# Passing first-choice results through the second choices' rows: a GNN and mixture-of-experts kernel with one scatter less per token

## The chip, the cores and the metric

The kernel runs on one core of one Trainium2 chip. The time is that of the device, in microseconds, from the start of one execution to its end. The median of three runs of the kernel before is 489.01 us (488.24 to 489.42).

## The reference

8192 tokens of 128 features, in 128 graphs of 64 nodes, pass through two residual blocks. All is float32.

```python
x = x + gnn(layernorm(x), adj)     # adjacency product, 128->512, RMS norm, SiLU, 512->128
x = x + ffn(layernorm(x))          # mixture of 8 experts, each token uses its 2 best

def ffn(xf):
    top_w, top_i = top_k(xf @ Wg + bg, 2)
    top_w = softmax(top_w)
    w_dense = sum(one_hot(top_i, E) * top_w[..., None], axis=1)
    for e in range(E):
        h = gelu(xf @ W1[e] + b1[e])
        out = out + w_dense[:, e:e+1] * (h @ W2[e] + b2[e])
```

Below, `x2` is the sum after the first block. A token's result is `x2` plus its first choice's weighted output plus its second choice's weighted output.

## The kernel before, in words

There are two stages. In the token stage a loop over 16 groups of 512 tokens (`s`, with each step working on several groups at once) computes the first block, the gate scores, the two best experts of each token and, by prefix sums on TensorE (`prefix`), a row number for each token and choice. For each choice k there is an array in HBM, `dispatched_rows{k}`, with a region for each expert. GpSimd scatters each token's row to it with an indirect DMA of 128 rows, `dispatch(g, j, k)`. A row holds the token's number, the two weights, mean and reciprocal deviation for the second layer norm, and x2: 133 numbers, 532 bytes. That is 4 dispatches a group and choice, 128 in all. The first choices' dispatches of a group follow it by two steps. The second choices' ones are spread, three a step from step 3 on, and the other 22 between the tiles of the next stage (`second(n)`).

In the expert stage a tile is 128 rows of one expert. There are 71 tiles (TILES) for the first choices, numbered 0 to 70, and 71 for the second choices, 71 to 141 (NT = 142). Which expert and which row a tile begins with stands in tables that VectorE computes: `early_row` and `early_expert` for the first 40 tiles (EARLY), which can be full tiles of the first 12 groups and so start before all is dispatched; `row_tab` and `expert_tab` for the others. Places of a region's last tile that hold no token are padded with rows whose token number is out of bounds (`pad`), so that their writes are dropped.

The work of a tile i on its engines, each with its own queue in program order:

- SyncE, `load_slots(i)`: waits until slot buffer i % 16 (RING) is free, which is when the write of tile i - 16 has landed (`added`), reads the tile's row from the table, and loads 128 rows to `slot_rows`.
- VectorE: `norm_slots(i + 4)` (L1035), `copy_block(i + 3)` (L1029, first-layer weights and biases of the tile's expert), then `finish(i)`: L1115 adds the bias to the second layer's result, and L1122 (first choices: times weight, plus x2) or L1125 (second choices: times weight) writes `y_out`.
- TensorE: transpose of tile i + 1 (L661), first layer of tile i (L668, 4 matmuls), second layer of tile i - 1 (L683, 4 matmuls). A float32 matmul stands as two records in the trace.
- ScalarE: copies the transpose, and applies Gelu.
- GpSimd, `write_tile(i)`: L437, an indirect DMA that scatters 128 results of 512 bytes to `out`, for the first choices; L440, the same with an addition to what is in `out`, for the second choices. An addition must not start before the first choice's result of the same token is there, so GpSimd waits for all first choices' writes ahead of tile 71 (`wait_written`).

The end of the kernel waits on SyncE for all writes.

## Time and profile before

| what | us |
|---|---|
| median of the runs | 489.01 |
| the profiled execution, its own time | 488.13 |
| its span, first to last instruction | 486.2 |
| TensorE busy (matmul) | 465.9, 96% of the span |
| VectorE busy | 354.1 |
| GpSimd busy | 353.4 |
| 71 accumulating writes, L440 | 112.6, 1.586 each |
| 71 plain writes, L437 | 72.2, 1.017 each |
| 128 dispatches, L425 | 126.0, 0.985 each |

Start with the end of the span and go back: what is the last thing that runs, and since when is it alone. Then ask for each stretch which engine has no idle time. GpSimd's share of 73% is an average over stretches: it is busy 8 tenths of each slice in the last third, up to the last slice, in which all other engines are still. The TensorE clock granted is full in all slices but the last.

### The profile page before, as it was taken

To read this page: it belongs to the slowest core of one execution; us is meant where nothing else is said; L and a number is where in the kernel's file an instruction comes from. 1 tells how busy PE (TensorE), PEld (TensorE's weight loads), DVE (VectorE), ACT (ScalarE), POOL (GpSimd) and SP (SyncE) were. 2 spreads that over 40 slices of the span, in tenths; PEclk is the share of its full clock that TensorE was granted. 3 is DMA by queue.
4 is the path that set the end of the run, shared out by engine and by line. 5 is a ranking of instruction groups with operands and counts; after the bars stand their busy time and mean duration, and the time that the engine had idled before them with its cause. 6 is when DMAs were issued, how large, how long until landed. Compare 5 with 4: busy or idle time off the path is not lost.

```text
span 486.2 us, 14184 instructions
## 1 busy us (share of the span) xinstructions
PE 465.9 (96%) x3715; PEld 422.8 (87%) x3715; DVE 354.1 (73%) x1484; ACT 264.2 (54%) x830; POOL 353.4 (73%) x310
## 2 busy tenths in 40 slices
PE   8999999999999999999999999999999999999960
PEld 6788888778888777899999999999999999999950
DVE  6798888888887675888867777777667676776730
ACT  2333333333333324677777777777777777777730
POOL 3232587877778777777777777777588888888884
PEclk9999999999999999999999999999999999999995
DMA  6995122222222212323334333333254555555430
GB/s 188 361 320 168 56 79 73 79 77 64 68 64 68 78 40 74 86 70 90 96 91 108 100 104 98 93 85 99 47 68 68 72 72 76 70 69 73 56 33 5
DMA packets 54436, 44.78 MB, mean 92 GB/s; under 512 B 9506, under 2 KB 46024, under 8 KB 54360
## 3 DMA queue, kind: packets, MB, share of 16 engines
q1 hardware_dynamic: 36480, 26.11, 20.0%
q0 software_dynamic: 16592, 17.13, 17.5%
q8 instruction: 35, 0.57, 0.5%
q10 hardware_dynamic: 1288, 0.62, 0.4%
q14 instruction: 41, 0.34, 0.2%
HBM read 25.49 MB, written 19.25 MB: 92 GB/s over the span
## 4 chain that ended last, share of the span: by engine, by line
PE 67%; POOL 15%; issue 14%; DVE 1%; ACT 1%; POOLq 1%
PE ps L683 14%; PE ps L668 14%; POOL out_y L440 14%; PE ps L589 11%; PE ps L575 10%; PE ps L541 3%; PE ps L549 3%; PE ps L582 3%; PE ps L557 2%; PE ps L661 2%; PE ps L567 1%; POOL dispatched_rows L425 1%; PE ps L500 1%; POOLq L71 1%; PE ps L612 0%
## 5 line engine op out<-in xcount | busy, mean ns | idle before, releaser
L775 ACT ACTIVATE gelu_t<-ps,block_w 128x128 f32<-128x128 f32 x568 | 162.5, 369 | 35.1 <-PE ps L668 34.7
L425 POOL DMA_INDIRECT dispatched_rows<-payload,row_idx x128 | 126.0, 985 | 37.3 <-issue 36.7
L668 PE MATMUL ps<-slot_t,block_w 128*128 128x128 f32 x1136 | 150.1, 275 | 0.6 <-ACT slot_t L769 0.6
L683 PE MATMUL ps<-experts,gelu_t 128*128 x1136 | 150.3, 275 | 0.4 <-ACT gelu_t L775 0.3
L683 PEld LDWEIGHTS ps<-experts,gelu_t 128*128 128x128 f32 x1136 | 138.2, 192 | 0.8 <-issue 0.8
L668 PEld LDWEIGHTS ps<-slot_t,block_w 128*128 128x128 f32 x1136 | 138.0, 192 | 0.9 <-ACT slot_t L769 0.9
L440 POOL DMA_INDIRECT out_y<-y_out,slot_rows x71 | 112.6, 1586 | 23.3 <-issue 23.3
L437 POOL DMA_INDIRECT out_y<-y_out,slot_rows x71 | 72.2, 1017 | 24.1 <-issue 19.0
L1115 DVE TENSOR_TENSOR y_bias<-ps,block_w 128x128 f32<-128x128 f32 x142 | 41.3, 291 | 52.8 <-PE ps L683 48.1
L1029 DVE COPY block_w<-experts 128x644 f32 x142 | 73.6, 519 | 2.0 <-issue 2.0
L1035 DVE TENSOR_SCALAR slot_n<-slot_rows 128x128 f32<-128x128 f32 x142 | 58.5, 413 | 15.5 <-DMA slot_rows<-dispatched_rows 15.1
L589 PE MATMUL ps<-w2e,hidden 128*128 128x136 f32 x512 | 69.6, 279 | 0.0
L589 PEld LDWEIGHTS ps<-w2e,hidden 128*128 128x128 f32 x512 | 63.9, 190 | 0.0
L732 ACT ACTIVATE hidden<-ps,vec_cols 128x512 f32<-128x512 f32 x64 | 44.0, 687 | 32.8 <-PE ps L575 32.7
L575 PE MATMUL ps<-agg_r,w1b 128*128 128x512 f32 x128 | 59.1, 603 | 0.0
L769 ACT COPY slot_t<-ps 128x128 f32<-128x128 f32 x142 | 37.7, 266 | 34.4 <-PE ps L661 34.2
L414 POOL TENSOR_TENSOR powers<-powers_in,neg_half 128x12 f32<-128x12 f32 (+2 forms) x17 | 33.9, 1993 | 23.9 <-DVE powers_in L838 23.2
L575 PEld LDWEIGHTS ps<-agg_r,w1b 128*128 128x128 f32 x128 | 23.0, 190 | 22.6 <-issue 22.5
L661 PE MATMUL ps<-ident,slot_n 128*128 128x128 f32 x142 | 38.6, 273 | 0.0
L745 ACT ACTIVATE agg<-ps,ones 128x512 f32<-128x512 f32 x16 | 11.0, 687 | 50.4 <-PE ps L541 50.4
L582 PEld LDWEIGHTS ps<-ident_wg,xs_t 128*128 128x128 f32 x128 | 20.5, 190 | 13.9 <-issue 13.9
L1125 DVE TENSOR_SCALAR y_out<-y_bias,slot_rows 128x128 f32<-128x128 f32 x71 | 30.7, 432 | 2.5
(146 smaller groups left out, 413.3 us busy)
## 6 DMA issues: line engine op xcount, KB each, us to landing
slot_rows<-dispatched_rows SPq DMA_DIRECT2D x142, 66.5 KB
xs<-in_x SPq DMA_DIRECT2D x16, 256.0 KB, 6.5
xs_t<-in_x_t SPq DMA_DIRECT2D x16, 256.0 KB, 3.1
experts<-in_f_w SPq DMA_DIRECT2D x16, 256.0 KB, 5.3
out_y<-y_out,slot_rows POOLq DMA_INDIRECT x142, 3.2
adj_in<-in_adj_t SPq DMA_DIRECT2D x16, 128.0 KB, 4.3
dispatched_rows<-payload,row_idx POOLq DMA_INDIRECT x128, 2.4
dispatched_rows<-pad_rows SPq DMA_DIRECT2D x18, 66.5 KB
```

The costliest lines, as they stand in the source:

```text
L425: pool.indirect_dma_start(rows[k], bass.IndirectOffsetOnAxis(row_idx[:, g, j * TOP_K + k:j * TOP_K + k + 1], 0), payload[:, g * JT + j, 0: ...
L437: pool.indirect_dma_start(out, token, y_out[:, r, :], None, bounds_check=T - 1, oob_is_err=False).then_inc(added[r], 16)
L440: pool.indirect_dma_start(out, token, y_out[:, r, :], None, bounds_check=T - 1, oob_is_err=False, compute_op=ALU.add).then_inc(added[r], 16)
L575: pe.matmul(bank(n % H_BANKS, 0, GROUP), w1b[:, c * P:(c + 1) * P], agg_r[:, s % 2, :], start=True, stop=True).then_inc(h_done, 1)
L589: mm = pe.matmul(x2_part(j), hidden[:, c, j * P:(j + 1) * P], w2e[:, c, :], start=False, stop=(c == C - 1))
L661: pe.transpose(bank(TURN_BANK + i % 2, 0, P), slot_n[:, i % (AHEAD + 1), :], ident[:]).then_inc(slots_turned, 1)
L668: mm = pe.matmul(bank((2 * i + c // 2) % FH_BANKS, c % 2 * SLOTS, SLOTS), block_w[:, i % BLOCKS, c * P:(c + 1) * P], slot_t[:, i % 2, :], ...
L683: mm = pe.matmul(bank(Y_BANK + i % 2, 0, P), gelu_t[:, i % 2, c, :], experts[:, bass.ds(at + (OW2 + c * P), P)], start=(c == 0), stop=(c = ...
L732: act.activation(hidden[:, c, :], ps[:, (C * s + c) % H_BANKS, :], ACT.Silu, scale=vec_cols[:, GRW + c:GRW + c + 1]).then_inc(hidden_ready, 1)
L775: act.activation(gelu_t[:, i % 2, c, :], ps[:, (2 * i + c // 2) % FH_BANKS, c % 2 * SLOTS:(c % 2 + 1) * SLOTS], ACT.Gelu, bias=block_w[:, ...
L1029: dve.tensor_copy(block_w[:, i % BLOCKS, :], experts[:, bass.ds(at, OW2)]).then_inc(block_ready, 1)
L1035: dve.tensor_scalar(slot_n[:, i % (AHEAD + 1), :], row[:, X2:WID], row[:, MEAN:MEAN + 1], row[:, RSTD:RSTD + 1], ALU.subtract, ALU.mult).t ...
```

## The change

A first choice's result no longer goes to `out`. Instead, the whole slot row with the result behind it (262 numbers, 1048 bytes) is scattered to the row of a new array `forwarded_rows` at which the token's second choice has its place. The place travels in the row (`PLACE`, so a row has 134 numbers). A second choice's tile loads such rows, which hold x2, statistics, weights and the first choice's result, adds its own part on VectorE, and writes the final result to `out` with a plain scatter. The accumulating write and GpSimd's waits for earlier writes are gone.

So that the expert stage needn't stand still between the choices, the second choices of the first four groups (SECOND_GROUPS) are still dispatched from the token stage, 16 dispatches, and give 8 full tiles (SECONDS), 71 to 78. Their slots are loaded from `dispatched_rows1`, and the first choices' results for them come later from `forwarded_rows` by a load of their own, `load_prior`, 512 bytes a row. VectorE keeps their second-layer result in the slot (`take_second`) and closes them later (`close_second`): one at tile 75, then two in each of tiles 76 to 79. The early tables are computed for both choices.

```diff
             def write_tile(i):
                 r = i % RING
                 pool.wait_ge(y_ready, i + 1)
-                token = bass.IndirectOffsetOnAxis(slot_rows[:, r, TOKEN:TOKEN + 1].bitcast(I32), 0)
                 if i < TILES:
-                    pool.indirect_dma_start(out, token, y_out[:, r, :], None, bounds_check=T - 1,
+                    place = bass.IndirectOffsetOnAxis(slot_rows[:, r, PLACE:PLACE + 1].bitcast(I32), 0)
+                    pool.indirect_dma_start(forwarded, place, slot_rows[:, r, :], None, bounds_check=DUMMY - 1,
                                             oob_is_err=False).then_inc(added[r], 16)
                 else:
-                    pool.indirect_dma_start(out, token, y_out[:, r, :], None, bounds_check=T - 1,
-                                            oob_is_err=False, compute_op=ALU.add).then_inc(added[r], 16)
-
-            def wait_written(i):
-                pool.wait_ge(added[i % RING], 16 * (i // RING + 1))
+                    token = bass.IndirectOffsetOnAxis(slot_rows[:, r, TOKEN:TOKEN + 1].bitcast(I32), 0)
+                    pool.indirect_dma_start(out, token, slot_rows[:, r, WID:FWD], None, bounds_check=T - 1,
+                                            oob_is_err=False).then_inc(added[r], 16)
...
-                if s >= SECONDS_FROM:
-                    second(3 * (s - SECONDS_FROM))
+                if 0 <= 2 * (s - SECONDS_FROM) < SECOND_GROUPS * JT:
+                    second(2 * (s - SECONDS_FROM))
+                    second(2 * (s - SECONDS_FROM) + 1)
...
-                n = SECONDS_LEFT + (i - 1) // 5 * 2 + (i % 5 == 3)
-                if i % 5 in (1, 3) and n < G * JT:
-                    second(n)
-
-
-                if TILES - 8 <= i < TILES - 1:
-                    wait_written(2 * i - TILES)
-                    wait_written(2 * i - TILES + 1)
-                if i == TILES:
-                    wait_written(TILES - 2)
-                    wait_written(TILES - 1)
                 write_tile(i)
...
-            sp.wait_ge(second_dispatched, 16 * JT * G)
-            for i in range(TILES, NT):
+            sp.wait_ge(second_dispatched, 16 * JT * SECOND_GROUPS)
+            firsts = [load_slots(i) for i in range(TILES, TILES + SECONDS)]
+
+
+            for i in range(TILES + SECONDS - RING, TILES):
+                sp.wait_ge(added[i % RING], 16 * (i // RING + 1))
+            for i in range(TILES, TILES + SECONDS, 2):
+                load_slots(SECONDS + TILES + (i - TILES) // 2)
+                load_prior(i, firsts[i - TILES])
+                load_prior(i + 1, firsts[i + 1 - TILES])
+            for i in range(TILES + SECONDS + SECONDS // 2, NT):
                 load_slots(i)
...
+                dve.tensor_copy(payload[:, cols(g), PLACE].bitcast(I32),
+                                row_f[:].rearrange("p (j k) -> p j k", k=TOP_K)[:, :, 1])
                 dve.tensor_copy(row_idx[:, g, :], row_f[:]).then_inc(rows_ready, 1)
...
+            def take_second(i):
+
+                dve.wait_ge(y_done, i + 1)
+                dve.tensor_tensor(slot_rows[:, i % RING, X2:WID], ps[:, Y_BANK + i % 2, 0:P],
+                                  block_w[:, i % BLOCKS, OB2:OB2 + P], ALU.add).then_inc(y_chain, 1)
+
+            def close_second(i):
+                row = slot_rows[:, i % RING, :]
+                dve.wait_ge(y_chain, i + 1)
+                if i < TILES + SECONDS:
+                    dve.wait_ge(prior_loaded[i - TILES], 16)
+                dve.scalar_tensor_tensor(row[:, WID:FWD], row[:, X2:WID], row[:, WEIGHT + 1:WEIGHT + 2],
+                                         row[:, WID:FWD], ALU.mult, ALU.add).then_inc(y_ready, 1)
...
+                if i == TILES + 4:
+                    close_second(TILES)
+                if TILES + 5 <= i <= TILES + SECONDS:
+                    close_second(2 * i - TILES - 9)
+                    close_second(2 * i - TILES - 8)
+                if i > TILES + SECONDS:
+                    close_second(i)
```

GpSimd's queue from the last writes of the first choices on; the bracket holds the semaphores waited for. Before:

```order
L437 DMA out_y<-y_out,slot_rows 8192x128 [waits y_ready,added2,added1]
L437 DMA out_y<-y_out,slot_rows 8192x128 [waits y_ready,added4,added3]
L437 DMA out_y<-y_out,slot_rows 8192x128 [waits y_ready]
L440 DMA out_y<-y_out,slot_rows 8192x128 [waits y_ready,added6,added5]
L440 DMA out_y<-y_out,slot_rows 8192x128 [waits y_ready] x70
```

And in the changed kernel, from the last dispatches on:

```order
L472 DMA forwarded_rows<-slot_rows 66688x262 [waits y_ready] x11
L460 DMA dispatched_rows<-payload,row_idx 66688x134 [waits rstd_stored,rows_ready]
L472 DMA forwarded_rows<-slot_rows 66688x262 [waits y_ready]
...
L472 DMA forwarded_rows<-slot_rows 66688x262 [waits y_ready] x57
L476 DMA out_y<-slot_rows 8192x128 [waits y_ready] x71
```

GpSimd no longer waits for writes, and between the tiles only the last group's four dispatches are left, behind tiles 10 to 13.

SyncE's queue at the turn between the choices: the loads of tiles 78 and 79. `TENSOR_LOAD` reads a table. Before:

```order
L290 TENSOR_LOAD row_tab [waits added14]
L290 ISA x2
L341 ISA
L341 DMA slot_rows<-dispatched_rows 128x133
L290 TENSOR_LOAD row_tab [waits added15]
```

And in the changed kernel:

```order
L302 TENSOR_LOAD early_row [waits added14]
L302 ISA x2
L358 ISA
L358 DMA slot_rows<-dispatched_rows 128x134
L302 TENSOR_LOAD row_tab [waits added4,added3,added5,added2,added6,added1,added15,added0]
L302 ISA x2
L361 ISA
L361 DMA slot_rows<-forwarded_rows 128x262
L367 ISA
L367 DMA slot_rows<-forwarded_rows 128x128
L367 ISA
L367 DMA slot_rows<-forwarded_rows 128x128
```

The wait for one write has become a wait for eight (and by the loads ahead of it for all 71), and two loads of priors follow each of four slot loads.

VectorE at tile 76 of the changed kernel; before, a tile had one L1115 and one L1125 in place of the last three rows:

```order
L1068 TENSOR_SCALAR slot_n<-slot_rows 128x128 [waits slots_turned,slots_loaded0]
L1062 ISA [waits y_done,y_chain]
L1062 COPY block_w<-experts 128x644
L291 TENSOR_LOAD expert_tab
L291 ISA x2
L1162 TENSOR_TENSOR slot_rows<-ps,block_w 128x128 [waits y_done]
L1170 SCALAR_TENSOR_TENSOR slot_rows<-slot_rows 128x128 [waits prior_loaded1,y_chain]
L1170 SCALAR_TENSOR_TENSOR slot_rows<-slot_rows 128x128 [waits prior_loaded2,y_chain]
```

The normalisation of tile 80 stands first and waits for its load; two closings that wait for priors stand last.

## Rows read from the trace of the kernel before

**Rows 1.** Busy time by stretch: window, length, PE, PEld, DVE, ACT, POOL, clock, DMA.

```profile
202.00:336.00 134.00, 134.00 (x1208) 133.85 (x1207) 102.42 (x334) 99.04 (x353) 103.60 (x102) 1.00 0.35 95
346.00:470.00 124.00, 123.39 (x1105) 123.02 (x1103) 85.16 (x257) 90.92 (x323) 103.34 (x65) 1.00 0.50 66
```

**Rows 2.** Timeline of the end: start us, length us, engine, line, operation [idle before].

```profile
467.18 2.25 PE L683 MATMUL ps<-experts,gelu_t 128*128 x16
...
469.80 0.29 DVE L1125 TENSOR_SCALAR y_out<-y_bias,slot_rows 128x128 f32<-128x128 f32 x1
470.01 1.55 POOL L440 DMA_INDIRECT out_y<-y_out,slot_rows  x1 [0.30 <-issue]
...
479.28 1.55 POOL L440 DMA_INDIRECT out_y<-y_out,slot_rows  x1 [0.30 <-issue]
```

**Rows 3.** GpSimd's indirect DMAs by line: ns min/median/max, first and last start; landing.

```profile
L437 POOL DMA_INDIRECT out_y<-y_out,slot_rows x71: 978/992/1320, 214.9 to 343.9; - x71
...
DMA to landing us min/median/max: 2.1/2.4/4.2
...
L440 POOL DMA_INDIRECT out_y<-y_out,slot_rows x71: 1549/1554/1657, 346.9 to 479.3; - x71
...
L425 POOL DMA_INDIRECT dispatched_rows<-payload,row_idx x128: 957/962/1262, 47.9 to 317.8; - x128
...
out_y<-y_out,slot_rows POOLq DMA_INDIRECT x6, 2.7
```

**Rows 4.** DMA view, windows 60:178 and 346:470: packets, MB, share; issues, landing.

```profile
q0 software_dynamic: 2336, 4.98, 12.6%
...
dispatched_rows<-payload,row_idx POOLq DMA_INDIRECT x74, 2.4
...
q0 software_dynamic: 9216, 4.01, 36.0%
...
out_y<-y_out,slot_rows POOLq DMA_INDIRECT x65, 3.4
```

**Rows 5.** Timeline at the turn: tile 70's result, tile 79's normalisation and transpose.

```profile
336.01 0.35 DVE L1122 SCALAR_TENSOR_TENSOR y_out<-y_bias,slot_rows 128x128 f32<-128x128 f32 x1
...
343.79 0.39 DVE L1035 TENSOR_SCALAR slot_n<-slot_rows 128x128 f32<-128x128 f32 x1
...
346.85 0.27 PE L661 MATMUL ps<-ident,slot_n 128*128 128x128 f32 x1
```

**Rows 6.** Slot loads: SyncE's issues, a normalisation that waited, landing, and all waits.

```profile
250.11 0.34 SPq L341 DMA_DIRECT2D slot_rows<-dispatched_rows  x1
...
252.17 0.61 DVE L1035 TENSOR_SCALAR slot_n<-slot_rows 128x128 f32<-128x128 f32 x1 [1.14 <-DMA slot_rows<-dispatched_rows]
...
275.18 2.58 SPq L341 DMA_DIRECT2D slot_rows<-dispatched_rows  x3
...
xs_t<-in_x_t SPq DMA_DIRECT2D x9, 256.0 KB, 3.0
...
DVE slot_n L1035 <- DMA slot_rows<-dispatched_rows: 15.1, 17, 1.8
```

**Rows 7.** Timeline of a group in the token stage: GpSimd's power, TensorE's transposes of it.

```profile
114.11 2.33 POOL L414 TENSOR_TENSOR powers<-powers_in,neg_half 128x12 f32<-128x12 f32 x1 [0.34 <-DVE powers_in L838]
...
117.04 0.60 PE L567 MATMUL ps<-ident,powers 128*128 128x128 f32 x4
```

**Rows 8.** Timeline behind the early table: VectorE's ranks and TensorE's sums of squares.

```profile
179.19 0.23 DVE L904 TENSOR_TENSOR row_cand<-ps,next_row 128x64 f32<-128x64 f32 x1 [0.38 <-PE ps L603]
...
179.76 1.02 PE L557 MATMUL ps<-ones,prod 128*128 128x1 f32 x8 [0.61 <-DVE next_row L907]
```

**Rows 9.** Timeline of the expert stage's start: tile 0's result, the last power.

```profile
202.87 0.35 DVE L1122 SCALAR_TENSOR_TENSOR y_out<-y_bias,slot_rows 128x128 f32<-128x128 f32 x1
...
205.80 0.17 DVE L867 TENSOR_SCALAR powers_in<-payload 128x4 f32<-128x4 f32 x1
...
208.17 1.17 POOL L414 TENSOR_TENSOR powers<-powers_in,neg_half 128x4 f32<-128x4 f32 x1
```

More of the change, by code:

```diff
@@ L252, in moe_gnn @@
         added = [sem(f"added{r}") for r in range(RING)]
+        prior_loaded = [sem(f"prior_loaded{i}") for i in range(SECONDS)]
         def q_bank(g):
@@ L979, in early_table_2 @@
[L979 to L983 removed]
+                tables.link(dve.tensor_scalar(tile_row[:], tile_row[:], tile_first[:, 0:1], None, ALU.add))
```

135 lines of the change are left out of this document (81 added, 54 removed).

## Prediction

> **What bounds the kernel now.** I read the stretches first. In the first choices' tiles TensorE is busy for all of 134.00 us, in the second choices' for 123.39 of 124 us [rows 1]. The tile pace is therefore TensorE's: from the first tile's result to the last first choice's, 202.87 to 336.01 us, are 70 tiles of 1.902 us [rows 5, 9]. No engine can shorten the kernel inside these stretches unless it takes work from TensorE, and the change takes none.
>
> Then I read the end. The last second-layer matmuls start at 467.18 us and VectorE's last scaling at 469.80 us lasts 0.29 us, so all results are there at 470.09 us. At that time GpSimd is issuing an earlier tile's accumulating write (470.01 us), and five more follow, the last at 479.28 us [rows 2]. The kernel ends with 9.2 us in which only GpSimd's queue moves. The reason is its price: an accumulating write holds GpSimd for 1.554 us at the median, and with the gap of 0.30 us that stands before each one [rows 2] that is 1.85 us, against a tile every 1.90 us. GpSimd can just follow, but never catches up what it was behind at the turn between the choices. A plain scatter takes 0.992 us, 1.29 us with the gap [rows 3].
>
> **The change at the end: what it removes.** The second choices' 71 accumulating writes become plain ones. With 1.29 us a tile against 1.90 us GpSimd idles 0.6 us a tile and is waiting for the last result. Before, from the last write's start to the span's end are 486.2 - 479.28 = 6.92 us, of which 2.7 us is that write's landing and 4.2 us what comes after [rows 2, 3]. After: the last scaling becomes a fused multiply and add of two tiles, 0.35 us as L1122 takes it [rows 5], so the result is there at 469.80 + 0.35 = 470.15 us, the write starts at 470.2 us, lands 2.4 us later [rows 3], and 4.2 us follow: 476.8 us. Gain 9.4 us.
>
> **Dispatch.** 64 second-choice dispatches shrink to 16, so 48 x (0.96 + 0.30) = 60 us leave GpSimd [rows 3]. They lay beside TensorE's work, in stretches where it waited for nothing of theirs: worth nothing by itself. But it lets GpSimd start the tiles' writes earlier, which matters at the turn below.
>
> **The first half, VectorE.** Each group gets one more 128x4 cast ahead of L920, 0.1 to 0.2 us. It stands in a chain that ends in GpSimd's power (114.11 + 2.33 = 116.44 us), for which TensorE's transposes wait at 117.04 us [rows 7]. The slack is 0.6 us and the chain is set anew by TensorE in every group, so the copies don't add up: 0. The copy of the counts after group 3 adds about 0.2 us once, within the same slack. The early table's second part grows by four operations and one link, some 0.5 us; there TensorE already waited 0.6 us in front of L557, for L907. VectorE had 0.38 us of waiting of its own ahead of L904, which takes up most of the growth [rows 8]. I take 0.2 us; bounds 0 and 0.5.
>
> **The turn.** This is the new wait. From tile 79 on (the second choices' ninth tile), slots come from rows that the first choices' tiles wrote, of any tile, so SyncE waits for all 71 of their writes, and then issues in a row: load 79, two priors, load 80, two priors, and so on. Eight tiles (71 to 78), which come from the direct dispatch, cover it. Timed against the old schedule: tile 70's result is there at 336.01 + 0.35 = 336.36 us [rows 5]. GpSimd, without backlog, starts its scatter at 336.4 us. It landed in 2.4 us for 512-byte rows [rows 3]; a row is now 1048 bytes, and I add 0.4 us, between 0 and the 0.9 us that lie between the direct loads of 66.5 KB (250.11 to 252.17 us, 2.06 us) and of 256 KB (3.0 us) [rows 6]. So 339.2 us. SyncE's loads follow each other at 1.12 us (three in 2.58 us, the last one's 0.34 us taken off, by two), of which 0.34 us is the issue and 0.78 us the reading of the table [rows 6]: load 79 issues at 340.0 us and, 134 KB long, takes 2.06 + 0.4 us: 342.5 us.
>
> It is wanted by the normalisation that stands at 343.79 us, when VectorE gets to it: 1.3 us to spare. And VectorE may be late: TensorE's transpose of tile 79 stands at 346.85 us, and the first layer of tile 78, whose weights VectorE copies after that normalisation, follows it in TensorE's order; less 0.9 us for the two instructions of VectorE (0.39 us and the copy's 0.5 us) that is 346.0 us [rows 5]. In all 3.5 us of cover. That lateness of VectorE costs nothing is seen: it waited 17 times, up to 1.8 us, for slot loads in the first choices' tiles, while TensorE stayed fully busy [rows 1, 6].
>
> The burst behind it: a prior load reads no table, so it costs between 0.34 us (issue alone) and 1.12 us (like any load) [rows 6]. I take 0.45, as it has only the address arithmetic more than the issue. Then a round of load, prior, prior is 2.0 us against one tile of 1.90 us, as each tile wants one load more. Over the four rounds SyncE loses 0.4 us of its 1.3 us margin: covered. At 1.12 us each a round is 3.4 us, and load 83 would be 4 x 1.5 = 6 us behind against 1.3 + 2.2 us of cover: a stall of 2.5 us. That is the upper bound. VectorE does two closings in each of four tiles: 0.35 us more a tile for the second, where it idles 0.6 us a tile (38.8 of 124 us, by 65 tiles) [rows 1]. Covered.
>
> **Sum.** 9.4 - 0.2 = 9.2 us. The profiled execution would have a span of 477.0 us. That execution took 488.13 us and the median of the runs is 489.01 us, so I put the saving on the median: **479.8 us**.
>
> **Rival 1: the turn leaks.** Priors as dear as loads, or scattered 1048-byte rows that land as slowly as the slowest scatter (4.2 us instead of 2.4) [rows 3], use up the 3.5 us. TensorE would show a gap of 1 to 5 us near 347 to 353 us. Time 481 to 485 us. For it: twelve transfers in a row on one queue and one wait for all. Against it: rows 6 as worked out above. Chance 0.13.
>
> **Rival 2: a long row is priced like an accumulate.** The trace has no scatter of 1048-byte rows. The nearest: rows of 532 bytes (dispatch, 0.962 us) and 512 bytes (0.992 us) have the same price, so it isn't bytes, at that distance [rows 3]. What sets the accumulate apart is its packets: 2336 for 74 dispatches, 32 each, against 9216 for 65 writes, 142 each [rows 4]. That is 0.57 us for 110 packets, 5.2 ns a packet. If a row of 1048 bytes went out as a packet of its own, the scatter would take 1.55 us. GpSimd starts the first tile's scatter late: the last power's input is there at 205.97 us, it takes 1.17 us, and two dispatches of 1.26 us follow, so 209.7 us against a result at 203.2 us [rows 9], 6.5 us; four late dispatches add 5.0 us. At 1.85 us a tile against 1.90 only 3.6 of these 11.5 us are made good by tile 70: its scatter starts 8 us late and lands 1.6 us later still. Less 3.5 us of cover TensorE stalls 6 us: 485.8 us. I take 0.98 us for the scatter, as both plain rows agree; any price under 1.48 us costs nothing. Chance 0.07.
>
> The Trainium skill bears on this in "DMA: Bandwidth & Descriptors", section "SWDGE vs HWDGE vs iDMA": a packet preferably holds no more than 4096 bytes. An engine's eight rows of 1048 bytes would by that make three packets instead of one, and by this case's price per packet an estimate of 1.15 us, for which the forecast stands. The 532-byte rows, eight of which are 4256 bytes, still went in 32 packets per dispatch [rows 4], so the trace does not show that limit bite.
>
> **Rival 3, slower: the price of a scatter grows with its bytes.** Twice the bytes, 1.96 us, and with the gap 2.26 us against 1.90: GpSimd falls behind by 0.36 us in every tile of the first choices, 26 us, on top of the 11.5 us. The 16 slots or the wait for all writes pass this to TensorE: 11.5 + 26 + 1 - 3.5 = 35 us, 515 us. It decides from 1.61 us a scatter on, where the stall equals the 9.2 us. Between 1.48 and 1.61 us it is a smaller gain. Against it: the two row sizes above. Chance 0.06, to which all prices over 1.61 count.
>
> **Rival 4: nothing much.** The end is set by something other than GpSimd's backlog, or the change's copies cost TensorE 0.6 us in each group (9 us): 488 to 490 us. Against it: the six lone writes [rows 2] and the slack in rows 7. Chance 0.03.
>
> **Chances and range.** Forecast 0.68 (478.6 to 481), rival 1 0.13, rival 2 0.07, rival 3 0.06, rival 4 0.03, and 0.03 that it is under 478.6, if the closing stretch shrinks too. The range 478.4 to 483.5 us takes in the forecast's own and most of rival 1: 0.8. A measurement of this kernel can tell 0.3%, 1.5 us, from no change. Faster by more than that: forecast, rival 1, below, and most of rival 2, 0.89. Within: 0.04. Slower: 0.07.
>
> **What the profile after would show.** GpSimd's last write starting within 0.2 us of the last result, and the span ending 6 to 7 us behind it. The scatter of the first choices at 0.98 to 1.15 us. TensorE busy for the whole of 337 to 355 us. VectorE's waits for priors and for load 79 under 2 us. If instead the scatter shows over 1.48 us, rival 2 or 3 holds; if TensorE has a gap at the turn with cheap scatters, SyncE's burst is the step that failed; if TensorE has gaps before 180 us, it is the copies.

## The result and the profile after

| | before | after |
|---|---|---|
| time, median of 4 runs each on one chip | 489.22 us (488.24 to 490.25) | 477.11 us (476.44 to 477.35) |
| ratio | | 0.975, 95% interval 0.972 to 0.977 |
| span of the profiled execution | 486.2 us | 475.6 us |
| from the last write's start to the span's end | 6.92 us | 3.78 us |

The change is worth 12.1 us, where 9.2 were forecast: the right side, but 1.3 us below the range. (The runs of three experiments, named at their place, fell on chips where the kernel before itself takes 608 to 609 us; their times are compared only with each other.)

The stretches of the kernel after (window, length, busy time of PE, PEld, DVE, ACT, POOL, clock, DMA share, GB/s) answer to [rows 1]; the middle one is the turn:

```profile
202.00:336.00 134.00, 133.68 (x1204) 133.67 (x1205) 98.85 (x334) 99.10 (x356) 77.83 (x78) 1.00 0.42 119
336.00:346.00 10.00, 10.00 (x92) 10.00 (x92) 5.17 (x17) 7.35 (x27) 1.96 (x2) 1.00 0.23 56
346.00:470.00 124.00, 123.96 (x1112) 123.78 (x1110) 85.25 (x261) 91.16 (x324) 68.27 (x69) 1.00 0.38 104
```

TensorE is as full as before, and for all of the turn. GpSimd went from 103.60 to 77.83 us and from 103.34 to 68.27 us. The end, as [rows 2] (start us, length us, engine, line, operation, idle before):

```profile
470.26 0.29 DVE L1162 TENSOR_TENSOR slot_rows<-ps,block_w 128x128 f32<-128x128 f32 x1 [0.51 <-PE ps L702]
470.54 0.98 POOL L476 DMA_INDIRECT out_y<-slot_rows  x1 [0.81 <-DVE slot_rows L1170]
470.58 0.35 DVE L1170 SCALAR_TENSOR_TENSOR slot_rows<-slot_rows 128x128 f32<-128x128 f32 x1
471.82 0.98 POOL L476 DMA_INDIRECT out_y<-slot_rows  x1 [0.30 <-issue]
```

Six lone accumulating writes have become one plain write. The last result is there at 470.93 us, its write starts 0.89 us later. GpSimd's DMAs by line (ns min/median/max, first and last start; landings), as [rows 3]:

```profile
L472 POOL DMA_INDIRECT forwarded_rows<-slot_rows x71: 978/980/1334, 211.0 to 337.9; - x71
...
L476 POOL DMA_INDIRECT out_y<-slot_rows x71: 977/978/1280, 347.3 to 471.8; - x71
...
forwarded_rows<-slot_rows POOLq DMA_INDIRECT x71, 2.6
out_y<-slot_rows POOLq DMA_INDIRECT x71, 2.4
```

What lies behind the last write is not in the timeline, since DRAIN is not counted as busy work. It shows among the instructions of the block's own line, in which every engine closes (operation, ns min/median/max, start). Of the kernel before:

```profile
L71 POOLq DRAIN  x1: 15361/15361/15361, 470.6 to 470.6; - x1
L71 SPq COMPARE_BRANCH  x1: 41/41/41, 482.2 to 482.2; - x1
...
L71 SPq EVENT_SEMAPHORE  x1: 17/17/17, 486.2 to 486.2; - x1
```

and of the kernel after:

```profile
L77 POOLq DRAIN  x1: 3817/3817/3817, 471.5 to 471.5; - x1
L77 SPq COMPARE_BRANCH  x1: 41/41/41, 474.1 to 474.1; - x1
...
L77 SPq EVENT_SEMAPHORE  x1: 17/17/17, 475.5 to 475.5; - x1
```

SyncE's program ends by waiting for every write, so its branch marks the last landing: 482.2 us before, 474.1 us after. GpSimd's DRAIN then still lasts until 470.6 + 15.36 = 486.0 us before, 3.8 us behind the last landing, and until 471.5 + 3.82 = 475.3 us after, 1.2 us behind it. From here on "the tail" is the time from the end of GpSimd's last DMA instruction to the end of its DRAIN: 486.0 - (479.28 + 1.55) = 5.1 us before, 475.3 - (471.82 + 0.98) = 2.5 us after. The forecast had it as a constant.

### The profile page after: what moved, and what is told of

The parts are those of the page before. It is cut to its first block, busy times and chain, and to the rows that moved or that the text cites. A ratio compares the mean times of both kernels' runs of the same rounds, so it can differ in the third digit from the quotient of the medians.

```text
span 475.6 us, 14020 instructions
## 1 busy us (share of the span) xinstructions
PE 466.6 (98%) x3715; PEld 423.8 (89%) x3715; DVE 350.5 (74%) x1504; ACT 263.7 (55%) x830; POOL 262.3 (55%) x262
## 3 DMA queue, kind: packets, MB, share of 16 engines
q0 software_dynamic: 8240, 18.29, 11.2%
## 4 chain that ended last, share of the span: by engine, by line
PE 93%; issue 2%; DVE 2%; POOL 1%; ACT 1%; POOLq 0%
PE ps L702 27%; PE ps L687 26%; PE ps L594 10%; PE ps L608 10%; PE ps L560 3%; PE ps L680 3%; PE ps L568 3%; PE ps L601 3%; PE ps L576 3%; PE ps L586 1%; PE ps L519 1%; POOL dispatched_rows L460 1%; PE ps L631 0%; PE ps L629 0%; POOL powers L449 0%
## 5 line engine op out<-in xcount | busy, mean ns | idle before, releaser
L476 POOL DMA_INDIRECT out_y<-slot_rows x71 | 70.2, 989 | 63.6 <-DVE slot_rows L1170 52.9
L472 POOL DMA_INDIRECT forwarded_rows<-slot_rows x71 | 70.6, 994 | 52.2 <-DVE slot_rows L1156 45.0
L460 POOL DMA_INDIRECT dispatched_rows<-payload,row_idx x80 | 79.0, 987 | 22.8 <-issue 22.1
L1062 DVE COPY block_w<-experts 128x644 f32 x142 | 70.6, 497 | 2.0 <-issue 2.0
L1162 DVE TENSOR_TENSOR slot_rows<-ps,block_w 128x128 f32<-128x128 f32 x71 | 20.7, 292 | 41.1 <-PE ps L702 40.3
L1068 DVE TENSOR_SCALAR slot_n<-slot_rows 128x128 f32<-128x128 f32 x142 | 49.3, 348 | 0.3
L1152 DVE TENSOR_TENSOR y_bias<-ps,block_w 128x128 f32<-128x128 f32 x71 | 20.7, 291 | 32.4 <-PE ps L702 31.3
```

The source lines that it names most:

```text
L460: pool.indirect_dma_start(rows[k], bass.IndirectOffsetOnAxis(row_idx[:, g, j * TOP_K + k:j * TOP_K + k + 1], 0), payload[:, g * JT + j, 0: ...
L472: pool.indirect_dma_start(forwarded, place, slot_rows[:, r, :], None, bounds_check=DUMMY - 1, oob_is_err=False).then_inc(added[r], 16)
L476: pool.indirect_dma_start(out, token, slot_rows[:, r, WID:FWD], None, bounds_check=T - 1, oob_is_err=False).then_inc(added[r], 16)
L1062: dve.tensor_copy(block_w[:, i % BLOCKS, :], experts[:, bass.ds(at, OW2)]).then_inc(block_ready, 1)
L1068: dve.tensor_scalar(slot_n[:, i % (AHEAD + 1), :], row[:, X2:WID], row[:, MEAN:MEAN + 1], row[:, RSTD:RSTD + 1], ALU.subtract, ALU.mult).t ...
```

## The experiments

### What shortens the tail: the kind of write, the backlog, or neither

Two runs separate the two halves of the change. The first makes all of the old kernel's writes plain, so it leaves out the addition, and keeps its 270 indirect DMAs:

```diff
-                    pool.indirect_dma_start(out, token, y_out[:, r, :], None, bounds_check=T - 1,
-                                            oob_is_err=False, compute_op=ALU.add).then_inc(added[r], 16)
+                    pool.indirect_dma_start(out, token, y_out[:, r, :], None, bounds_check=T - 1,
+                                            oob_is_err=False).then_inc(added[r], 16)
```

> The kernel before, with the second choices' 71 writes plain instead of accumulating, and nothing else changed (all dispatches and waits stand). It leaves out the addition: a token's result is its second choice's part alone. Theory A (the whole gain comes from the price of the accumulating write, at the end of the kernel): GpSimd keeps up, the last write starts some 0.8 us behind the last result at 470.1 us and the span ends 3.8 us later as in the changed kernel, at 474.7 us; time 12 us under before, about 477 us. By the prediction's old term (6.6 us from the last write's start to the end) it would be 2.8 us more, 479.5 us. Rival (part of the gain comes from the 48 dispatches or the waits that are gone): it stays above the changed kernel by 1 us or more beyond that.

The second makes the 71 final writes of the new kernel accumulate (each adds to what the output held, so those sums are not the reference's):

```diff
                     pool.indirect_dma_start(out, token, slot_rows[:, r, WID:FWD], None, bounds_check=T - 1,
-                                            oob_is_err=False).then_inc(added[r], 16)
+                                            oob_is_err=False, compute_op=ALU.add).then_inc(added[r], 16)
```

> The changed kernel, with the second choices' 71 writes accumulating again (the sums in the output are then wrong). Theory A: GpSimd gets a backlog at the turn, since nine closings come within 9 us and it needs 1.85 us each: 9 x 1.85 = 16.7 us against 7 us, so 8 to 10 us behind, of which 62 tiles win back 0.05 us each, 3 us: 5 to 7 us behind at the end, and the last write's start is followed by 6.9 us instead of 3.8: 8 to 10 us over the changed kernel, 485 to 487 us. Rival: the end is set by something else, then less than 4 us.

Measured: 482.16 us (ratio 0.985, 0.982 to 0.987) and 486.66 us (0.994, 0.991 to 0.996). The second is as expected. The first is 5 us over its expectation, with a timeline that ends as forecast. The old kernel with plain writes, its last two writes and then its closing line:

```profile
470.61 0.98 POOL L440 DMA_INDIRECT out_y<-y_out,slot_rows  x1 [0.85 <-DVE y_out L1125]
471.89 0.98 POOL L440 DMA_INDIRECT out_y<-y_out,slot_rows  x1 [0.30 <-issue]
```

```profile
L71 POOLq DRAIN  x1: 8670/8670/8670, 471.5 to 471.5; - x1
L71 SPq COMPARE_BRANCH  x1: 41/41/41, 474.2 to 474.2; - x1
```

The last write starts within 0.1 us of the kernel after's and has landed at 474.2 us, yet the DRAIN ends at 480.2 us: a tail of 7.3 us. The queue's 7.4 us are won and 2.2 of them lost again in the tail. So plain writes alone don't make the tail short. This run has a plain last write and no backlog (GpSimd stands idle for 0.85 us ahead of the last write but one), and its tail is the longest so far. That speaks against both theories on record: the kind of the last write, and the backlog of DMAs that GpSimd still has at the end. Both were also asked directly. For the kind, only the last tile's write was changed, in either kernel:

```diff
-                if i < TILES:
+                if i < TILES or i == NT - 1:
```

(This is the edit of the kernel before, in which it makes the last write plain. In the kernel after, the last write alone, i == NT - 1, becomes accumulating.)

> The changed kernel, with only the last tile's write accumulating (that tile's sums are then wrong). It asks why the time from the last write's start to the end fell from 6.9 to 3.8 us. Theory K (GpSimd's closing drain takes longer behind a write of the accumulating kind): +3.1 us, about 480.2 us, and the drain ends some 5 us behind the write. Theory Q (the drain is long because it was queued behind a backlog): only the write's own 0.57 us and 0.3 us of landing, +0.9 us, 478.0 us. Theory N (it grows with the number of accumulating writes in the kernel): also +0.9 us or a little more.

> The kernel before, with only the last tile's write plain (that tile leaves out the addition). GpSimd's backlog stays as it is, so the last write starts at 479.3 us of the span. Theory K (kind of the last write): the drain is short, the span ends 3.8 us after that start, 3.1 us under before, about 486 us. Theories Q (backlog) and N (number of accumulating writes): only 0.9 us under before, about 488.3 us.

Measured: 477.72 us and 489.00 us (ratio 0.999, 0.997 to 1.000). The tails are 2.6 us (after, last write accumulating) and 5.2 us (before, last write plain), against 2.5 and 5.1 us: the kind of the last write is not it. The last tile holds padding rows alone, whose writes are dropped (the last two writes of the kernel after move 0.00 MB), so these two runs say nothing on a last write with data.

For the backlog, GpSimd of the kernel after waits for the last result before it issues the last seven writes:

```diff
             for i in range(NT):
+                if i == NT - 7:
+                    pool.wait_ge(y_ready, NT)
```

> The changed kernel, in which GpSimd waits for the last result before it issues the writes of the last seven tiles, so that seven plain writes stand at the end. Their last starts 6 x 1.28 = 7.7 us later than in the changed kernel. Theory K (the drain is long only behind an accumulating write): +7.7 us, 484.8 us, with 3.8 us from the last start to the end. Theory Q (the drain is long behind a backlog): 2.5 to 3 us more, 487.5 us.

Measured: 484.71 us, the last write at 479.12 us, and this closing line:

```profile
L77 POOLq DRAIN  x1: 8130/8130/8130, 474.5 to 474.5; - x1
L77 SPq COMPARE_BRANCH  x1: 41/41/41, 481.4 to 481.4; - x1
```

A tail of 474.5 + 8.13 - 480.10 = 2.5 us, as without the backlog. The backlog theory falls. What the kernels with tails of 5 to 7 us have in common is that they issue 270 indirect DMAs.

### The dispatches that were worth nothing

The kernel after with all 64 second dispatches back at their old places; the 48 more write rows that nobody reads. GpSimd then issues 270 indirect DMAs instead of 222.

```diff
-                if 0 <= 2 * (s - SECONDS_FROM) < SECOND_GROUPS * JT:
-                    second(2 * (s - SECONDS_FROM))
-                    second(2 * (s - SECONDS_FROM) + 1)
+                if s >= SECONDS_FROM:
+                    second(3 * (s - SECONDS_FROM))
...
+                if s >= SECONDS_FROM:
+                    second(3 * (s - SECONDS_FROM) + 1)
+                    second(3 * (s - SECONDS_FROM) + 2)
...
+                n = 3 * (G + 1 - SECONDS_FROM) + (i - 1) // 5 * 2 + (i % 5 == 3)
+                if i % 5 in (1, 3) and n < G * JT:
+                    second(n)
```

> The changed kernel with all 64 second-choice dispatches put back at the places they had before; the 48 put back write rows that no tile reads. It tells what 60 us less on GpSimd were worth. The prediction says nothing: within 0.5 us of the changed kernel, 477.1 us. Rival: GpSimd is behind at the turn or its descriptors slow the others, 1 us or more.

Measured: 484.79 us (0.991, 0.989 to 0.993), 7.7 us more than the kernel after. Its end, its closing line, and the only wait of TensorE in it that the kernel after doesn't have:

```profile
472.93 0.98 POOL L476 DMA_INDIRECT out_y<-slot_rows  x1 [0.81 <-DVE slot_rows L1175]
474.21 0.98 POOL L476 DMA_INDIRECT out_y<-slot_rows  x1 [0.30 <-issue]
```

```profile
L77 POOLq DRAIN  x1: 8635/8635/8635, 473.9 to 473.9; - x1
L77 SPq COMPARE_BRANCH  x1: 41/41/41, 476.5 to 476.5; - x1
```

```profile
PE ps L685 <- DVE slot_n L1073: 0.9, 1, 0.9
```

Two losses. The tail is 473.9 + 8.64 - 475.19 = 7.3 us instead of 2.5. And the last write starts 2.4 us later. The wait of 0.9 us is only part of this; the rest shows in the starts of TensorE's transposes, one a tile:

```profile
257.55 0.34 DVE L1073 TENSOR_SCALAR slot_n<-slot_rows 128x128 f32<-128x128 f32 x1 [2.09 <-DMA slot_rows<-dispatched_rows]
257.95 0.33 PE L685 MATMUL ps<-ident,slot_n 128*128 128x128 f32 x1 [0.94 <-DVE slot_n L1073]
```

From 254.50, 257.95 and 264.06 us to the next transpose are 3.45, 2.32 and 2.30 us instead of 1.90, at full granted clock: 2.4 us in all. Ahead of each of the three VectorE had waited for a slot load (1.2, 2.1 and 1.6 us); in the kernel after it stands idle for 0.3 us in all ahead of its 142 normalisations. The loads were late because their slots were: between 200 and 270 us SyncE waits 16.2 us in all, up to 4.3 us at a time, for forwarded rows to land, against 6.3 us in the kernel after, and GpSimd, which writes those rows, has no gap over 0.31 us in its queue from 250 to 267 us. Put together with the three kernels above:

| | last write starts | tail | time |
|---|---|---|---|
| accumulating, 270 DMAs (before) | 479.28 | 5.1 | 489.22 |
| accumulating, 222 (second run) | 478.96 | 3.6 | 486.66 |
| plain, 270 (first run) | 471.89 | 7.3 | 482.16 |
| plain, 270, dispatches back (this run) | 474.21 | 7.3 | 484.79 |
| plain, 222 (after) | 471.82 | 2.5 | 477.11 |

Taking the 48 dispatches out of the changed kernel is worth 7.7 us; this pair differs in nothing else. The other pairs with 270 and 222 DMAs differ by 489.22 - 486.66 = 2.6 us with accumulating writes and by 482.16 - 477.11 = 5.1 us with plain ones, but there the forwarding of rows differs too.

### Does the tail follow the count?

The next runs add dispatches to the kernel after. The first four put them behind tile 74, one ahead of each write (shown for 24; 36 and 48 alike), and in one 90 over both halves of the expert stage, 42 of them to a spare table:

```diff
             for i in range(NT):
                 if LAST_FIRSTS <= i < LAST_FIRSTS + JT:
                     dispatch(G - 1, i - LAST_FIRSTS, 0)
+                n = SECOND_GROUPS * JT + i - 75
+                if 75 <= i and n < SECOND_GROUPS * JT + 24:
+                    second(n)
                 write_tile(i)
```

> The kernel after with 24 more second dispatches (groups 4 to 9, to rows that nobody reads), one ahead of each write of tiles 75 to 98: 246 indirect DMAs on GpSimd instead of 222. Nothing of the computation is left out. Measured quantity: from the end of GpSimd's last write (its DMA instruction) to the end of its closing DRAIN; 2.5 us at 218 and 222 of them, 7.3 us at 270. Theory L (grows evenly with the count, 0.1 us for each above 222): 4.9 us, span about 478.0. Theory S (a step somewhere between 222 and 270): either 2.5 us (span 475.6) or 7.3 us (span 480.4). Theory M (the place of the dispatches in the program matters, not their number): 2.5 us.

> As the run with 24 more, with 36 more second dispatches (groups 4 to 12), one ahead of each write of tiles 75 to 110: 258 indirect DMAs. Nothing is left out. From the last write's end to the DRAIN's end: theory L 6.1 us (span 479.2), theory S 2.5 or 7.3 us, theory M 2.5 us.

> As the run with 24 more, with all 48 more second dispatches (groups 4 to 15), one ahead of each write of tiles 75 to 122: 270 indirect DMAs, as many as in the run that had them at their old places, but all behind the turn. Nothing is left out. Theories L and S: 7.3 us from the last write's end to the DRAIN's end; theory M: 2.5 us. TensorE: at their old places they went with a last result 2.4 us later; here, with nothing added before the turn, the last write should start at 471.8 again as in the kernel after. So L and S: span 480.4, time about 482 (ratio 0.985); M: span 475.6, time 477.1.

> The kernel after with 90 more dispatches: the 48 second ones, and 42 that write second choices' rows once more to a spare table that nobody reads, ahead of three of four writes in tiles 1 to 59 and 77 to 135: 312 indirect DMAs. Nothing is left out. From the last write's end to the DRAIN's end: theory L 11.5 us, span about 484.6 if TensorE's end stays; theory S 7.3 us, span 480.4; theory M not determined.

Measured: 487.95, 497.25, 511.53 (ratio 1.046, 1.042 to 1.050) and 529.98 us. Every expectation of the time was missed, and the trace says why. Timeline of GpSimd with 48 more, an early part of the second choices' tiles, and TensorE's waits between 380 and 480 us (us in total, times, longest):

```profile
384.49 0.96 POOL L460 DMA_INDIRECT dispatched_rows<-payload,row_idx  x1 [0.31 <-issue]
385.76 0.98 POOL L476 DMA_INDIRECT out_y<-slot_rows  x1 [0.30 <-issue]
387.04 1.02 POOL L460 DMA_INDIRECT dispatched_rows<-payload,row_idx  x1 [0.30 <-issue]
```

```profile
PEld ps L683 <- DVE slot_n L1071: 12.2, 18, 1.6
PE ps L683 <- DVE slot_n L1071: 8.3, 13, 1.4
```

One dispatch and one write are 387.04 - 384.49 = 2.55 us of GpSimd, and a tile is 1.90 us of TensorE. GpSimd falls 0.65 us behind in each tile; the ring of 16 slots passes it on: the write frees the slot that the load waits for, the load feeds the normalisation, the normalisation the transpose. Adding a DMA to each tile moves the bound from TensorE to GpSimd. The tails, 5.4 us at 246 DMAs, 6.6 at 258, 7.6 at 270, rise with the count, about as the even theory says from 222 on; but at 312 the tail was 2.4 us.

So four more runs, with the added DMAs spread thinly, on either side of where the tail falls back; shown is the one with 60 (12 in the token stage, one a step; 48 ahead of two of five writes, whose tiles stand in the list two_of_five; the edit is written shorter here than in the run). The last of them is the old kernel with plain writes and 36 added; it leaves out the addition, as the first run did.

```diff
+                if 2 <= s < 14:
+                    spare(next(spare_of))
...
+                if i in two_of_five:
+                    second(SECOND_GROUPS * JT + two_of_five.index(i))
                 write_tile(i)
```

> The kernel after with 12 more second dispatches to rows that nobody reads, one ahead of every fourth write from tile 80 to 124: 234 indirect DMAs on GpSimd. Nothing is left out. An indirect DMA with its wait takes GpSimd 1.28 us (0.98 and an idle 0.30); at one more in four tiles that is 1.6 us for a tile's 1.83 us of TensorE, so TensorE should lose nothing and the last write start at 471.8. Theory C (a count that falls back, 0.1 us for each above about 192): 4.2 us from the last write's end to the DRAIN's end, span 477.3. Theory L (even from 222): 3.7 us, span 476.8. Theory B (only a crowded GpSimd shows it): 2.5 us, span 475.6.

> The kernel after with 60 more dispatches: 12 to a spare table in the token stage (one a step), 48 second ones ahead of two of five writes in tiles 1 to 58 and 76 to 133: 282 indirect DMAs. Nothing is left out. At 1.79 us of GpSimd for a tile's 1.83 TensorE should lose at most some 2 us, as it did with 48 at their old places. From the last write's end to the DRAIN's end: theory C 9.0 us if it falls back above 282 (2.5 if below); theory L 8.5 us; theory B 7.3 us or less.

> As the run with 60 more, with 24 in the token stage instead of 12: 294 indirect DMAs. From the last write's end to the DRAIN's end: theory C 2.5 us (falling back at 288) or 10 us (falling back between 294 and 312); theory L 9.7 us; theory B like the run with 60 more.

> The kernel before with plain second writes (the second choices' addition to the first ones' results is left out, as in the run with all writes plain), and 36 more dispatches to a spare table: 3 and then 1 a step in the token stage, and one ahead of every third write from tile 75: 306 indirect DMAs instead of 270. With 270 it had 7.3 us from the last write's end to the DRAIN's end, span 480.4, 482.2 us. Theory C: 2.5 us, so that 36 more DMAs make it quicker: span 475.6 and 477.5 us, if TensorE's end stays (up to 3 us more if the fuller token stage delays it). Theory L: 10.9 us, span 484. Theory B: 7.3 us, span 480.4.

Measured: 478.30, 482.74, 490.63 and 491.20 us. Placed thinly the DMAs leave TensorE alone: with 12 it was busy for 94.00 of the 94 us from 346 to 440, with 60 for 93.88, and the last writes start at 471.45 and 472.80 us. With 72 it isn't the expert stage that loses but the token stage, which now holds 24 of them. The waits of TensorE in its first 200 us, and the step's order on GpSimd:

```profile
PE ps L596 <- POOL powers L450: 6.6, 8, 1.1
```

```profile
104.65 0.96 POOL L461 DMA_INDIRECT spare_rows<-payload,row_idx  x1 [0.31 <-issue]
105.91 1.04 POOL L461 DMA_INDIRECT spare_rows<-payload,row_idx  x1 [0.30 <-issue]
106.97 2.33 POOL L450 TENSOR_TENSOR powers<-powers_in,neg_half 128x12 f32<-128x12 f32 x1
```

One more DMA ahead of a step's power is free (with 60 more, TensorE's waits there are those of the kernel after), two are not. The room for it is GpSimd's own idle time ahead of the power. In the kernel after:

```profile
103.47 2.33 POOL L449 TENSOR_TENSOR powers<-powers_in,neg_half 128x12 f32<-128x12 f32 x1 [1.61 <-DVE powers_in L857]
```

One DMA with its gap, 1.26 us, fits into these 1.61 us; two, 2.52 us, overrun them by more than the 0.6 us of slack in [rows 7]. The closing lines with 12 and with 72:

```profile
L77 POOLq DRAIN  x1: 5125/5125/5125, 471.1 to 471.1; - x1
```

```profile
L77 POOLq DRAIN  x1: 8113/8113/8113, 479.4 to 479.4; - x1
```

All tails, each worked out as above from the DRAIN's row and the last write's:

| indirect DMAs | 218 | 222 | 234 | 246 | 258 | 270 | 282 | 294 | 306 | 312 |
|---|---|---|---|---|---|---|---|---|---|---|
| tail, plain writes, us | 2.5 | 2.5, 2.5 | 3.8 | 5.4 | 6.6 | 7.3, 7.3, 7.6 | 6.4 | 6.4 | 6.0 | 2.4 |

(218 is the run with four covering tiles, below.) At 270 the tail goes by the count and not by the place: it is 7.3 to 7.6 us with the additions at their old places, behind the turn, or in another kernel. But no theory on record fits: 3.8 and 5.4 us refute a single step, 282 and 294 refute both the even rise (8.5, 9.7) and the fall at 288 (9.0, 2.5), and 6.0 at 306 refutes 2.5. Above 270 each count was run once and in one placement, so that the decline goes by the count alone is not shown.

The last question was whether the tail is work that earlier DMAs have left, which could be done earlier:

```diff
+                if i == TILES:
+                    pool.drain()
                 write_tile(i)
```

> The kernel after with all second dispatches at their old places (270 indirect DMAs), and a DRAIN instruction on GpSimd in the turn, between the last forwarded scatter (done at 342.9) and the first final write (wanted at about 348). Nothing is left out. Theory W (the DRAIN works off what earlier indirect DMAs left behind, whenever it comes): the new DRAIN takes some us, up to 5 us more than the floor of about 2.5 us, and delays the first writes, which GpSimd makes good at 1.28 us a write against 1.83 us a tile; the closing DRAIN then ends 2.5 us behind the last write's end instead of 7.3, span 478.0, time about 480. Theory E (it stands only at the program's end and goes by all DMAs of the program): closing DRAIN 7.3 us behind the last write's end, span 482.8, time 484.8 as without it.

> The run with a DRAIN in the turn once more (270 indirect DMAs, 199 ahead of it and 71 behind it), beside the same kernel without it. Nothing is left out. Theory W (work left behind by earlier DMAs): closing DRAIN 2.5 us behind the last write's end, span 478.0. Theory E (it goes by the whole program's DMAs): 7.3 us and 482.8. On the chip with the low clock it was 5.9 us, and the DRAIN in the turn ended 6.1 us behind the DMA ahead of it: if that holds here, a DRAIN in the middle takes 1.4 us off the closing one at most, span about 481.4.

> The kernel after with all 64 second dispatches at their old places (270 indirect DMAs) once more, as the partner of the run with a DRAIN in the turn. Nothing is left out. All theories: 7.3 us from the last write's end to the closing DRAIN's end, span 482.8, time 484.8.

In these three TensorE's granted clock was 0.78 to 0.80 from 200 to 300 us, against 1.00 in the kernel before. The first took 618.11 us and its tail was 5.9 us. The other two, on one chip, took 617.79 with the DRAIN in the turn and 620.78 without. Closing lines with and without it:

```profile
L77 POOLq DRAIN  x1: 7154/7154/7154, 608.1 to 608.1; - x1
```

```profile
L77 POOLq DRAIN  x1: 8635/8635/8635, 611.1 to 611.1; - x1
```

Without it the tail is 7.3 us again, to the tenth, though the kernel runs 136 us longer: the tail is not a matter of TensorE's clock or of pace. With it the tail is 5.9 us (last write at 608.43 us), and the DRAIN in the turn took 7.28 us and ended 6.1 us behind the DMA ahead of it. The theory that the DRAIN works off what earlier DMAs left wanted 2.5, the theory that it goes by the whole program's DMAs 7.3; both fall. The DRAIN in the turn has 199 indirect DMAs ahead of it, fewer than the 218 and 222 that give 2.5 us at the end, and yet ends 6.1 us late. What sets the tail stays open.

### The turn

The forecast's largest structural risk was the turn. The cover was halved: three groups' dispatches and four covering tiles, 71 to 74.

```diff
-SECOND_GROUPS = 4
+SECOND_GROUPS = 3
...
-                if i == TILES + 4:
+                if i == TILES + SECONDS // 2:
...
```

> The changed kernel with the second choices of three groups dispatched instead of four: 4 tiles instead of 8 cover the turn. The first forwarded load was issued at 340.9 us of the span and wanted at 344.3 us; with four tiles less it is wanted 7.6 us earlier, at 336.7 us, while it can't be issued earlier. With 2.45 us for its landing it is there at 343.4 us. TensorE's own cover is 2.2 us, so it stalls for 4.5 us: 481.6 us, with TensorE idle near 340 to 345 us. Rival (the turn has more cover than worked out): under 2 us. Rival (the loads behind it are late too): over 7 us.

Measured: 482.39 us (0.986, 0.984 to 0.989), 5.3 us more than the kernel after, close to what was expected. The stretch and TensorE's one long wait:

```profile
336.00:346.00 10.00, 6.62 (x52) 6.25 (x52) 2.73 (x8) 4.23 (x15) 1.56 (x2) 0.94 0.24 56
```

```profile
PE ps L680 <- DVE slot_n L1068: 3.3, 1, 3.3
```

The wait is 3.3 us, but the last write starts 5.1 us later than in the kernel after. The rest is TensorE's clock: after the 3.3 us in which it stood idle, its granted clock fell from 1.00 to the lower of its two levels:

```profile
344.00:346.00 2.00, 2.00 (x15) 1.98 (x14) 1.04 (x3) 1.14 (x4) 0.00 (x0) 0.71 0.49 108
346.00:348.00 2.00, 2.00 (x11) 2.00 (x10) 1.00 (x4) 0.89 (x3) 0.00 (x0) 0.50 0.48 122
```

From 348.95 us on a tile takes 1.90 us again; the two before it, whose transposes start at 343.02 and 345.97 us, took 2.95 and 2.98, so the slower clock costs 2.1 us. (Together with the wait that is 0.3 us more than 5.1; ahead of the wait this run was 0.45 us earlier than the kernel after.)

So the turn's chain (last scatter, landing, SyncE, load) is what the prediction described, and four tiles of cover, 7.6 us, are too few by 3.3 us of TensorE's waiting. With eight, by this run, the margin is about 4.3 us, an estimate (7.6 - 3.3).

## Why the prediction was right and wrong

**The queue at the end: right.** GpSimd's lone writes went, and the writes alone account for it: between the runs with 222 DMAs the last write starts 7.1 us earlier when it is plain.

**What comes after the last landing: this term was mis-sized.** The sum put 2.4 us of landing and 4.2 us of "what comes after" behind the last write's start and measured 3.78 us in all, 2.8 us less. This size alone took the result out of the range: with 2.8 us more the median would have been 479.9 us. The 4.2 us were read as one span in the kernel before and carried over as fixed; the closing line shows 3.8 us of them as GpSimd's DRAIN, which outlasts the last landing by 1.2 us in the kernel after.

**"Worth nothing by itself": this step failed.** The 48 dispatches were costed by TensorE's stretches alone. With plain writes their removal shortens the tail from 7.3 to 2.5 us, and in the changed kernel it also has the last write start 2.4 us earlier. With them back at their old places the changed kernel gains 489.22 - 484.79 = 4.4 us, not 12.1 and not 9.2. In part this was luck: plain writes beside 270 DMAs lengthen the tail (7.3 us against 5.1), taking out 48 DMAs shortens it, and the forecast, which knew of neither, missed only the difference.

**The last write's start: 1.4 us too early.** The forecast was 470.2 us and 0.2 us for the table; it was 471.82, 0.89 us behind the last result and not the 0.2 us that the prediction named as a sign. Of this 0.6 us are there in the last result (470.93 instead of 470.35), and they come from the kernel's opening, not from the change: GpSimd's first power starts at 19.87 us in this execution and at 19.13 in that of before, and it starts at 18.80 to 19.87 us in the traces of kernels with the changed token stage. The other 0.8 us is GpSimd. The prediction let an idle GpSimd start with its releaser's end; here it stands 0.81 us idle behind the releaser of the last write but one, and the last write is queued behind that one (470.54 + 0.98 + 0.30 = 471.82).

**From span to median: 1.3 us.** The saving was put on the median of 489.01 us, while the profiled execution of before took 488.13. That of after took 477.35, against a median of 477.11. So 1.1 us of the gain is the choice of this base (0.88 and 0.24), and 0.2 us the distance of the span to its own execution's time (1.9 and 1.75 us). Together: 479.8 + 1.4 - 2.8 - 1.3 = 477.1 us.

**The price of a 1048-byte scatter: right.** 980 ns against the 0.98 taken, and a landing of 2.6 us against 2.8. The queue's line of the page of the profile, before 16592 packets and 17.13 MB, became

```profile
q0 software_dynamic: 8240, 18.29, 11.2%
```

More bytes and half the packets. The plain writes and dispatches go in 32 packets each (8640 for 270 in the old kernel with plain writes), so the 71 scatters of 1048-byte rows take 8240 - 151 x 32 = 3408, or 48 each, and the 71 accumulating writes had 16592 - 199 x 32 = 10224, or 144 each. A long row did not go out as a packet of its own, as rival 2 had it. And 16 packets more cost GpSimd nothing (980 against 978 ns), where rival 2's 5.2 ns a packet would give 0.08 us: what makes an accumulating write dear is not shown by the packets alone.

The estimate of 1.15 us by the Trainium skill ("DMA: Bandwidth & Descriptors", section "SWDGE vs HWDGE vs iDMA", a packet of preferably no more than 4096 bytes) is refuted for the price by the same 980 ns, and its 32 packets more are 16 in the trace.

**The turn: right, with one size off.** SyncE's rows (SPq is its queue) and the normalisation of tile 79, as [rows 5, 6]:

```profile
340.93 0.34 SPq L361 DMA_DIRECT2D slot_rows<-forwarded_rows  x1
341.46 0.86 SPq L367 DMA_DIRECT2D slot_rows<-forwarded_rows  x2
343.10 0.34 SPq L361 DMA_DIRECT2D slot_rows<-forwarded_rows  x1
...
344.26 0.34 DVE L1068 TENSOR_SCALAR slot_n<-slot_rows 128x128 f32<-128x128 f32 x1
```

Load 79 issues at 340.93 us (forecast 340.0; the last scatter started at 337.94 instead of 336.4). Landing by the prediction's 2.5 us at 343.4 us, it is there before 344.26 us, and the normalisation shows no wait. A load and two priors are 343.10 - 340.93 = 2.17 us, against the 2.0 taken: a prior costs 0.53 us (341.46 - 340.93), not 0.45. TensorE lost nothing, so rival 1 did not come.

**The early table: right.** TensorE waits 0.77 us there instead of 0.61, 0.16 us more against 0.2 taken [rows 8]:

```profile
180.65 1.02 PE L576 MATMUL ps<-ones,prod 128*128 128x1 f32 x8 [0.77 <-DVE next_row L926]
```

**The range.** The case that happened, "under 478.6, if the closing stretch shrinks too", had a chance of 0.03. The 4.2 us had no row of their own; they got one value and no bounds, where the other unknown costs had both.

## What to carry to other kernels

When a kernel's end is part of the sum, read the instructions of the closing line on every engine: the time behind the last landing can be an engine's DRAIN, and it can depend on work far from the end. Cost a GpSimd DMA at what it holds the queue for (1.28 us here, not 0.98), against the period of what waits for that queue, in each stage apart: one more a step was free, two cost TensorE 6.6 us in all, and one more a tile made GpSimd the bound. Price a wait of TensorE with the slower clock behind it: 3.3 us of waiting at the turn cost 2.1 us more. When a term of the sum has only a remainder for its source, give it both bounds.

## What the runs showed of the hardware

GpSimd's closing DRAIN ends 2.4 to 7.6 us behind its last indirect DMA. With plain final writes this tail is 2.5 us at 218 and 222 of them, rises by about 0.1 us for each to 7.3 us at 270, lies at 6.0 to 6.4 us from 282 to 306, and was 2.4 us at 312. With 71 of them accumulating it is 3.6 us at 222 and 5.1 us at 270. In the old kernel with plain writes the DMA queues carry 64 packets from 471 to 481 us, all of them of the last two writes, so the tail is no transfer that the trace shows. The shape would suit something cyclic, but no run shows what. The Trainium skill ("DMA: Bandwidth & Descriptors", section "SWDGE vs HWDGE vs iDMA") has GpSimd append its DMAs' descriptors to rings in SBUF; no run here shows their state. The Trainium skill's page "VectorE: DVE Perf Modes", section "The DRAIN you can't avoid", describes two other kinds of DRAIN, the flush behind each VectorE operation and those that the runtime puts around a kernel, of about 12 ns on every engine. The ones measured here stand at the line of the kernel's own block and take 7 ns on SyncE, but 3813 to 17790 ns on GpSimd.

A GpSimd that has caught up starts an indirect DMA 0.8 to 0.9 us behind the instruction that releases it; one that is queued starts 0.30 us behind the end of the one before. Row lengths of 512, 532 and 1048 bytes cost the same 0.96 to 0.99 us at the median.

In the run with four covering tiles TensorE's granted clock went from 1.00 to 0.50 (346 to 348 us) behind a wait of 3.3 us; from 350 us on it was 1.00 again. In the run with the dispatches back it stayed at 1.00 behind the wait of 0.9 us.
